# A ternary feed-forward on bf16 parts, and two changes in the attentions of a twelve-stage decoder kernel

## The reference

```
x = x + L0_attn(ln(x)); x = x + L0_xattn(ln(x), ctx); x = x + L0_ffn(ln(x))
x = x + L1_attn(ln(x)); x = x + L1_xattn(ln(x), ctx); x = x + L1_ffn(ln(x))
x = x + L2_attn(ln(x)); ...                            # and six more
```

```
Wq = sign(W/gamma) * min(round(|W/gamma|), 1),  gamma = mean(|W|) + 1e-6     # -1, 0 or 1
h = gelu(x @ Wq_fc.T)                          # 256 -> 1024 columns
h = layernorm(h) * ln_w + ln_b
out = h @ Wq_proj.T                            # 1024 -> 256 columns
```

```
q, k, v = x Wq + bq, x Wk + bk, x Wv + bv
out = softmax(mask(q k^T / 8)) v Wo + bo
```

## Time and profile before

| stage | from, to (us) | stretch | busy in it: PE, DVE, ACT, POOL (us) | clock |
|---|---|---|---|---|
| `l0x` | 250 to 430 | 300 to 400 | 99.62, 90.32, 61.76, 50.36 | 1.00 |
| `l0f` | 433 to 579 | 500 to 540 | 40.00, 21.70, 15.38, 0.00 | 1.00 |
| `l1a` | 580 to 759 | 630 to 730 | 99.26, 90.72, 61.45, 50.37 | 1.00 |
| `l1x` | 763 to 996 | | | |
| `l2a` | 1204 to 1577 | 1310 to 1350 | 40.00, 15.91, 16.09, 10.38 | 1.00 |
| `l2fa` | 1800 to 1948 | 1830 to 1930 | 98.79, 89.17, 76.63, 64.90 | 1.00 |
| `l3x` | 2329 to 2520 | 2380 to 2480 | 89.80, 87.88, 81.98, 44.62 | 1.00 |

### The profile page before, as it was taken

One profiled execution on the slowest core, in us unless ns is written; L12 is line 12 of the kernel. 1 busy time (PEld: TensorE's weight loads), 2 busy tenths in 40 slices (PEclk: granted clock), 3 DMA queues, 4 the chain that ended last, 5 costly groups with the idle time before them and its releaser, 6 DMA issues. The chain is left out here.

```text
span 2934.9 us, 48117 instructions
## 1 busy us (share of the span) xinstructions
PE 2558.6 (87%) x16117; PEld 1872.8 (64%) x16117; DVE 1775.3 (60%) x4091; ACT 1337.9 (46%) x3461; POOL 809.9 (28%) x627
## 2 busy tenths in 40 slices
PE   5998989999688779699998998977969888869997
PEld 2666756767455446467776776757955566449896
DVE  7876886588788634444444657873346588434443
ACT  2333654256777323434333445743432388324442
POOL 5533530054100134122211224641110044142222
PEclk8999999999877789799999999988989999889999
DMA  9001000000200423200001002042130300531110
GB/s 322 4 0 50 14 19 1 14 3 1 65 5 1 87 67 110 90 1 1 1 1 40 22 1 73 2 147 85 37 91 1 85 15 5 174 123 52 51 52 27
DMA packets 152052, 142.44 MB, mean 49 GB/s; under 512 B 59948, under 2 KB 136770, under 8 KB 151428
## 3 DMA queue, kind: packets, MB, share of 16 engines
q1 hardware_dynamic: 139668, 110.61, 12.9%
q0 software_dynamic: 10560, 27.19, 2.7%
q10 hardware_dynamic: 1584, 1.57, 0.2%
HBM read 98.14 MB, written 43.02 MB: 48 GB/s over the span
## 5 line engine op out<-in xcount | busy, mean ns | idle before, releaser
L962 POOL TENSOR_TENSOR room<-room 128x1024 f32<-128x1024 f32 x144 | 274.0, 1903 | 432.2 <-DVE room L895 431.9
L1435 PE MATMUL l3f_out<-room,Y 128*128 x624 | 141.1, 379 | 0.0
L889 DVE TENSOR_REDUCE room<-room 128x8 f32<-128x1024 f32 (+1 forms) x144 | 139.9, 971 | 0.7 <-ACT room L1038 0.7
L962 POOL TENSOR_TENSOR room<-room,Y 128x1024 f32<-128x1024 f32 x32 | 60.7, 1898 | 252.0 <-DVE Y L895 252.0
L1435 PEld LDWEIGHTS l3f_out<-room,Y 128*128 128x128 f32 x624 | 115.6, 190 | 14.1
L1036 ACT ACTIVATE room<-l2a_scores,Y 128x128 f32<-128x128 f32 x256 | 72.1, 381 | 86.6 <-DVE Y L881 86.6
L2478 POOL DMA_INDIRECT sorted_rows<-room,l1f_place_i x32 | 31.0, 968 | 279.7 <-DVE l1f_place_i L2189 270.8
L607 PE MATMUL l2a_proj<-room 128*128 128x256 f32 x384 | 97.5, 398 | 11.6 <-ACT room L986 11.6
L1036 ACT ACTIVATE room<-l1a_scores,room 128x128 f32<-128x128 f32 x256 | 71.6, 386 | 58.4 <-DVE room L881 58.4
L1036 ACT ACTIVATE room<-l0x_scores,room 128x128 f32<-128x128 f32 x256 | 70.7, 385 | 59.2 <-DVE room L881 59.2
L607 PEld LDWEIGHTS l2a_proj<-room 128*128 128x128 f32 x384 | 71.8, 196 | 24.7 <-issue 14.9
(11 more groups left out here) (842 smaller groups left out, 7084.3 us busy)
## 6 DMA issues: line engine op xcount, KB each, us to landing
sorted_rows<-head SPq DMA_DIRECT2D x1, 16640.0 KB, 57.2
room<-in_L_ffn_w SPq DMA_DIRECT2D x16, 1024.0 KB
room<-in_L_ffn_W SPq DMA_DIRECT2D x16, 1024.0 KB
Y<-sorted_rows SPq DMA_DIRECT2D x62, 130.0 KB
room<-in_ctx SPq DMA_DIRECT2D x24, 256.0 KB, 2.7
room<-sorted_rows SPq DMA_DIRECT2D x39, 130.0 KB
room<-results SPq DMA_DIRECT2D x8, 512.0 KB, 7.1
room<-in_L_ffn_routed_w SPq DMA_DIRECT2D x4, 512.0 KB
```

Source lines behind the costliest of these rows:

```text
L889: dve.tensor_reduce(rsum[:, u % 2, 0:SUMMED], p[:, u % (TURN + 1), 0:SUMMED, :], AX.X, ALU.add)
L962: pool.tensor_tensor(p[:, u % (TURN + 1), :, :], p[:, u % (TURN + 1), :, :], rinv[:, u % (TURN + 1), :].unsqueeze(2).to_broadcast([P, HEAD ...
L1435: mm = pe.matmul(obank[n % 2][:, 0:D], hT[:, n % 2, f, :], chip.room[:, bass.ds(at + (SLOT // 2 + f * D), D)], start=(f == 0), stop=(f == ...
```

## The change

Three edits. In attentions that are not small and have no separate context (the 64-wide self attention alone), the turned rows leave the evenly dealt list: those of group g+2 are turned in the last section of group g, after the fills that stand there. In the small attentions and in `sample` the zero product is dropped; the first of the two products on a set of partitions starts the sum instead. In the ternary feed-forward both ternary weights are kept in bf16, and each f32 operand of the two layers becomes three bf16 parts whose sum it is exactly: the value rounded to bf16, the rest rounded to bf16, and what is left. ScalarE makes the first part, VectorE the second, POOL the third; of a pair of hidden chunks POOL subtracts the first part for one and VectorE for the other. The scaled hidden chunk stays in a staging buffer of four chunks. The products run over the parts. The second layer of group t-2 now runs in step t, sequence by sequence between the first layer of group t and two chunk turns of group t-1, so there is one more step.

```diff
+    early = [] if small or ctxsrc else turns
+    body = [f for f in steady if f not in early]
...
-                here.extend((g + 1, f) for n, f in enumerate(steady) if n * 3 * PER // len(steady) == r * 3 + sec and (f[0] != "y" or g + 1 >= first_turned))
+                here.extend((g + 1, f) for n, f in enumerate(body) if n * 3 * PER // len(body) == r * 3 + sec and turned_rows(g + 1, f))
+            if g + 2 < PAIRS and r == PER - 1 and sec == 2:
+                here.extend((g + 2, f) for f in early if turned_rows(g + 2, f))
...
-                        pe.matmul(out[:, 0:P], chip.zeros_b[:, :], chip.ident_b[:, :], start=True, stop=False, skip_group_check=True)
...
-                                               start=False, stop=(o == 1), skip_group_check=True)
+                                               start=(o == 0), stop=(o == 1), skip_group_check=True)
...
+    PARTS = 3
+    STAGED = 4
...
-                        for kc in range(KC):
-                            mm = pe.matmul(hbank[c][:, :], y_of(g)[:, kc, j * P:(j + 1) * P], fcT[:, kc, c * 512:(c + 1) * 512],
-                                           start=(kc == 0), stop=(kc == KC - 1))
+                        for part in range(PARTS):
+                            for kc in range(KC):
+                                mm = pe.matmul(hbank[c][:, :], yp[:, g % 2, part, kc, j * P:(j + 1) * P], fcT[:, kc, c * 512:(c + 1) * 512],
+                                               start=(part == 0 and kc == 0), stop=(part == PARTS - 1 and kc == KC - 1))
...
                     if j == 0:
-                        for f in range(FC - 4, FC):
-                            wait_emptied(pe, ("h", g, f))
+                        pe.wait_ge(h_split, (g + 1) * FC)
...
-                        mm = pe.matmul(obank[j % 2][:, 0:D], hT[:, f, j * P:(j + 1) * P], projT[:, f, :], start=(f == 0), stop=(f == FC - 1))
+                        for part in range(PARTS):
+                            mm = pe.matmul(obank[j % 2][:, 0:D], hp[g % 2][:, part, f, j * P:(j + 1) * P], projT[:, f, :],
+                                           start=(f == 0 and part == 0), stop=(f == FC - 1 and part == PARTS - 1))
...
+                for t in range(NG + 2):
                     for j in range(GR):
+                        if t < NG:
+                            first_layer(t, j)
+                        if t >= 2:
+                            second_layer(t - 2, j)
+                        if 0 <= t - 1 < NG:
+                            turn_hidden(t - 1, 2 * j)
+                            turn_hidden(t - 1, 2 * j + 1)
...
+                        if j == 2 and t + 1 < NG:
+                            turn_rows(t + 1)
...
+                def split_y(g):
...
+                    for kc in range(KC):
+                        dve.wait_ge(y_first, KC * g + kc + 1)
+                        dve.tensor_tensor(yr[:, kc, :], bank[kc][:, :], yp[:, g % 2, 0, kc, :], ALU.subtract).then_inc(emptied[kc], 1)
+                    dve.drain()
+                    for kc in range(KC):
+                        dve.tensor_copy(yp[:, g % 2, 1, kc, :], yr[:, kc, :]).then_inc(y_second, 1)
...
+                def split_hidden(g, f):
...
+                    dve.wait_ge(h_first, n + 2)
+                    dve.tensor_tensor(hT[:, (f + 1) % STAGED, :], hT[:, (f + 1) % STAGED, :], hp[g % 2][:, 0, f + 1, :], ALU.subtract)
+                    dve.wait_ge(h_rest, n // 2 + 1)
+                    dve.tensor_copy(hp[g % 2][:, 1, f, :], hT[:, f % STAGED, :]).then_inc(h_second, 1)
+                    dve.drain()
+                    dve.tensor_copy(hp[g % 2][:, 1, f + 1, :], hT[:, (f + 1) % STAGED, :]).then_inc(h_second, 1)
...
+                        if t < NG and j:
+                            hidden_sums(t, j - 1)
+                        if t >= 2:
+                            add((t - 2) * GR + j)
...
+                        if 0 <= t - 1 < NG:
+                            split_hidden(t - 1, 2 * j)
...
+                        if j == 2 and t + 1 < NG:
+                            split_y(t + 1)
+                            if t + 2 < NG:
+                                normalise(t + 2)
+                    if t < NG:
+                        hidden_sums(t, GR - 1)
+                        normalise_hidden(t)
...
+                def split_head():
+                    for kc in range(KC):
+                        pool.wait_ge(y_first, kc + 1)
+                        pool.tensor_tensor(yr[:, kc, :], chip.head[:, kc, :], yp[:, 0, 0, kc, :], ALU.subtract)
...
+                def last_of_y(g):
+                    for kc in range(KC):
...
+                        pool.tensor_tensor(yp[:, g % 2, 2, kc, :], yr[:, kc, :], yp[:, g % 2, 1, kc, :], ALU.subtract).then_inc(y_split, 1)
+                def rest_of_hidden(g, f):
+                    pool.wait_ge(h_first, g * FC + f + 1)
+                    pool.tensor_tensor(hT[:, f % STAGED, :], hT[:, f % STAGED, :], hp[g % 2][:, 0, f, :], ALU.subtract).then_inc(h_rest, 1)
+                def last_of_hidden(g, f):
+                    pool.wait_ge(h_second, g * FC + f + 1)
+                    pool.tensor_tensor(hp[g % 2][:, 2, f, :], hT[:, f % STAGED, :], hp[g % 2][:, 1, f, :], ALU.subtract).then_inc(h_split, 1)
...
+                def first_of_hidden(g, f):
+                    for i in range(f, f + 2):
...
+                        if n >= STAGED:
+                            act.wait_ge(h_split, n - STAGED + 1)
+                        act.activation(hT[:, i % STAGED, :], bank[b][:, :], ACT.Identity, bias=w.v["b"][:, i:i + 1], scale=w.v["g"][:, i:i + 1]).then_inc(emptied[b], 1)
+                    act.drain()
+                    for i in range(f, f + 2):
+                        act.copy(hp[g % 2][:, 0, i, :], hT[:, i % STAGED, :]).then_inc(h_first, 1)
...
+                        if t < NG:
+                            gelu(t, j)
+                        if t >= 1:
+                            first_of_hidden(t - 1, 2 * j)
```

More of the change, by code:

```diff
@@ L110, in block_sb, with half_sb @@
         return self.sb(name, shape, dt, ctx)
+    def half_sb(self, name, shape, ctx):
+        n = 1
+        for d in shape[1:]:
+            n *= d
+        dims = "abcd"[:len(shape) - 1]
+        whole = self.block_sb(name, [shape[0], n // 2], F32, ctx).bitcast(BF16)
+        return whole.rearrange(f"p ({' '.join(dims)}) -> p {' '.join(dims)}", **dict(zip(dims, shape[1:])))
     def begin_block(self, w, after, y_in_use):
@@ L2911, in ternary_ffn_block @@
         bank_of = {("fc", 0, q): b for q, b in ((0, 1), (2, 3), (1, 0), (3, 2))}
-        for t in range(NG + 1):
-            if t == 0:
-                fills += [("proj", 0, q) for q in range(WT)]
-            else:
-                fills += [("h", t - 1, f) for f in range(FC)]
-            if t + 1 < NG:
-                fills += [("y", t + 1, kc) for kc in range(KC)]
+        for t in range(NG + 2):
+            for j in range(GR):
+                if 0 <= t - 1 < NG:
+                    fills += [("h", t - 1, 2 * j), ("h", t - 1, 2 * j + 1)]
+                if t == 0 and j == 1:
+                    fills += [("proj", 0, q) for q in range(WT)]
+                if j == 2 and t + 1 < NG:
+                    fills += [("y", t + 1, kc) for kc in range(KC)]
         place, count = {}, [0] * 4
@@ L3021, in _ @@
                     turn_fc(q)
[L3022 to L3023 removed]
+                for t in range(NG + 2):
                     for j in range(GR):
[L3025 to L3030 removed]
+                        if t < NG:
[5 more added lines that the diff above has]
+                            turn_hidden(t - 1, 2 * j + 1)
+                        if t == 0 and j == 1:
                             for q in range(WT):
                                 turn_proj(q)
[L3033 to L3041 removed]
+                        if j == 2 and t + 1 < NG:
+                            turn_rows(t + 1)
+                        if t == NG + 1 and j == 1 and head:
+                            for b in range(2):
+                                pe.wait_ge(emptied[b], count[b])
+                            head.turn(pe, bank)
             def copy_fc(eng, q):
@@ L3116, in _ @@
                 w.wait(dve)
-                if not first_turned:
-                    empty_y(0)
                 threshold(0)
@@ L3122, in _ @@
                     ternary(0, fc, slice(i * HALF_W, (i + 1) * HALF_W)).then_inc(fc_ready, 1)
+                if not first_turned:
+                    split_y(0)
                 for q in (0, 2, 1, 3):
@@ L3159, in _, with first_of_y @@
             @block.scalar
             def _(act):
-                def empty_y(g):
-                    wait_filled(act, ("y", g, 1))
-                    act.copy(yT[:, g % 2, 1, :], bank[1][:, :]).then_inc(emptied[1], 1)
+                def first_of_y(g):
+                    for kc in range(KC):
+                        if g >= first_turned:
+                            wait_filled(act, ("y", g, kc))
```

(5 more changed lines are left out.)

134 lines of the change are left out of this document (59 added, 75 removed).

## The result

The changed kernel takes 2933.4 us in the median of 20 runs, the kernel before 2927.1 on the same chip: ratio 1.0024, with a 95% interval of 1.0016 to 1.0032. It is 6 to 7 us slower; forecast were 16 off.

What follows compares the result with a forecast made beforehand. TensorE was taken to bound `l2a`, `l0f` nearly throughout, and most 16-wide attentions. Terms -18.4 - 6.0 + 8.4 = -16.0 us took the median from 2930.9 to 2915, range 2898 to 2928.

Steps and rivals of the forecast that it cites:

- Part 1: `l2a`: turning rows ahead removes the whole key projection stall, 11.6 us, and the clock drops behind it, 6.8: 18.4 off.
- Part 2: Four attentions and `l1x`: dropped zero products at 0.05 us each, 4.8 in three bound stages and 1.2 elsewhere: 6.0 off.
- where TensorE waits anyway: Zero products: the 32 in `l3x` and the 16 in `l1x` together counted as 1.2 us off.
- Part 3, the products: `l0f`: bf16 parts make a first layer 2.58 us and a second 2.57, weight loads hidden, 28 us less TensorE work.
- four drops of 1.7 at most, two in the sum: `l0f`: TensorE idles at four group ends; two clock drops of 1.7 add 3.4 us, four in the upper bound, 6.8.
- Part 3, the walk, +5.0 and 3.4: `l0f`, step by step: ends at 584.0 against 579.0, 5.0 us more; clock drops add 3.4, sum +8.4.
- 1.6 for waits on POOL: `l0f`, step that turns group 0: 25.4 us of VectorE's work plus 1.6 for waits on POOL, 27.0 in all.
- The page's rule: `l0f`: certain VectorE and reading GpSimd instructions exclude each other; 0.9 us a pair, 3.6 at four ends; only the subtraction counted.
- (c): Rival, `l0f`: VectorE and POOL take turns everywhere, a group goes from 30.4 to 39 us; 2949 us; chance 0.06.
- (d): Rival, `l2a`: early turns do nothing, copy still behind exponentials or stall moves to scores; 18.4 lost, 2933 us; chance 0.08.
- (a): Rival, `l0f`: chain shorter than priced, engines pipeline better, clock stays; stage near -5, kernel 2901.5 us; chance 0.25.
- (b): Rival, `l0f`: TensorE stays the bound, so the stage gains 28 us; kernel 2879 us; chance 0.04.

Runs made afterwards that it cites:

- kernel 4: Only the rows turned ahead in `l2a`, against the kernel before: ratio 0.9941 (0.9927 to 0.9955), 17.3 us faster; `l2a` 354.9 us.
- (8): Changed kernel with POOL's last parts of the hidden values left out: ratio 0.9991 to the kernel before, 9.7 us less than the changed kernel; `l0f` 153.5.
- kernel 9: Changed kernel, POOL told of a pair's second parts only when both are rounded: ratio 1.0014 (1.0004 to 1.0023) to the kernel before; `l0f` 168.2 us.
- kernel 7: Kernel before with only the new order of `l0f`, all operands f32: ratio 1.0029 (1.0017 to 1.0040) to the kernel before; `l0f` 149.8 us.
- kernel 5: Kernel before with only the 16 zero products of `l1x` dropped: ratio 1.0018 (1.0008 to 1.0029), 5.3 us slower; `l1x` 246.8 us.
- 1: The kernel before, unchanged, profiled a second time: 2939.3 us, span 2937.6; `l1f` 204.6, `l1x` 237.6.

## Why the prediction was wrong

*Part 1, -18.4: right.* -19.0 in the profile, 17.3 by the ratio of kernel 4. The copy stood ahead of the exponentials, nothing took its place, the clock held; group starts 43.3 apart, forecast 43.5.

*Part 2, -6.0: right in four stages, of the wrong sign in the fifth.* 0.06 for a product of the four attentions by spacing and 0.05 by ratio. But I put the 16 of `l1x` among those "where TensorE waits anyway", and counted them at half price, 0.4 us off. In `l1x` the clock moved with what was taken away (0.77 to 0.74), and 5 us were given back, about all that the other 128 had won. The prediction has no term for the clock of `l1x`. Nor are all stages with waits alike: `l3x`, where TensorE waits too, did not lose.

*Part 3, the products: right.* 2.59 and 2.62 us for 2.58 and 2.57, hidden weight loads. Of the 28 us of work taken from TensorE its busy time over the stage shows only 15.7 (135.45 to 119.75). The other 12 went to the clock, as far as the traces tell: it was granted at 0.86 in the mean where the kernel before has 0.97. I had allowed four drops of 1.7 at most, two in the sum.

*Part 3, the walk, +5.0 and 3.4: the step that failed.* Forecast and measured, in us:

| | forecast | after | without last parts (8) |
|---|---|---|---|
| first hidden turn, from the stage's start | 32.1 | 32.9 | 33.5 |
| step with group 0 | 27.0 | 32.6 | 27.9 |
| next | 30.4 | 31.7 | 30.8 |
| without row turns | 28.8 | 30.3 | 29.3 |
| without first layers, to the last statistics | 30.2 | 36.9 | 31.0 |

The mis-sized term is POOL's last parts. The prediction has the last step go at TensorE's pace, a pair every 3.5 us (0.87 of turns, 2.6 of second layer), and the last part of chunk 7 ready 6.4 after its turn. In truth a pair took 4.77 from POOL and VectorE, and the second layer waited 10.5 us. Behind that wait two sequences of second layer took 7.54 us for the 5.2 that I reckoned, at a clock of 0.71 over 586 to 594 us; 4.1 and 2.3 are nearly all of the 6.7 that the last step is over. In the first step I counted VectorE's work and "1.6 for waits on POOL"; the measured excess is 5.6, and there TensorE waits 5.6 for the turned rows' last parts, which stand in POOL's queue behind the hidden chunks. I had summed each engine's work and checked it against the step, but had not closed the ring between two engines, whose length is the sum over both. Opening and steps are 15.9 us over the walk in all; with the walk's own 5.0 that is the 21.0 measured.

*The page's rule.* The Trainium skill, "SBUF — State Buffer", section "Who interferes with whom", said that the second rounding too would wait; the trace and kernel 9 agree (1425 against 427 ns). Its price as I worked it out, 3.6 us at four ends, would not have mended the forecast: kernel 9 shows that with the rounding free the time stays within what can be measured.

*The rivals.* (c) had the mechanism, VectorE and POOL in turns, but put it on all of VectorE's work at 39 us a group; it held in the split alone, at 31.7. (d)'s 2933 was met, for none of its reasons. In (a) and (b) I gave 0.29 to a chain shorter than priced; it was longer. The 21 us of `l0f` divide by the traces into the order (5.4, kernel 7), splitting without the last parts (3.7, from 149.8 to 153.5, after all that TensorE saves) and the last parts (11.9; 9.7 by the ratios). These are differences of single executions.

## What to carry to other kernels

Before a bound engine's work is cut, write down the chain of one unit (here a pair of chunks) through all engines and back to the buffer or queue it frees: if that ring or the chain at a group's end is longer than what will be left of the bound engine's work, the cut buys waits, and the waits buy a slower clock. Take the saving that adds the least to the others: splitting two chunks of rows a group, with the adds moved out of the way, took 4 us off the stage, where splitting the eight hidden ones too had put 21 on it. And in a stage where TensorE waits, do not drop small products as free of charge; time the edit there by itself.

## What the runs showed of the hardware

- Fewer products, more time: without 16 zero products `l1x` has 9 us more of busy TensorE, the granted clock 0.74 for 0.77 (kernel 5 against 1).
- A wait of 1.93 us of TensorE in `l2a` of the kernel before was followed by a lower clock in four of six cases, at 1.7 us each; without the waits (changed kernel, groups 43.29 us apart) the clock stayed at 1.00.
- A 128x512 f32 subtraction of POOL takes 1.16 us, whether it writes f32 or bf16, and 1.60 where a subtraction of VectorE's began just before it (571.59 and 571.77 us in the changed kernel). Where POOL's began first (567.01 and 567.48), VectorE's is the long one, 1.23 for 0.64 at the least. VectorE's rounding beside a last part of POOL's takes 1.42 for 0.42.
- A pause of TensorE, VectorE and ScalarE in the same microseconds of `l1f`, 5.5 to 8.8 us on TensorE, stands in 15 of 16 traces and is missing in one; what decides it was not tried.
